# Products of 64 rows in the chunked linear attention of a four-stage kernel

## What is computed

```python
def step(S, inp):
    rt, dt, kt, vt, at, bt = inp
    sa = jnp.einsum('bhij,bhj->bhi', S, at)
    S = S * dt[:, :, None, :] + sa[..., None] * bt[:, :, None, :] + vt[..., None] * kt[:, :, None, :]
    y = jnp.einsum('bhij,bhj->bhi', S, rt)
    return (S, y)
```

## Time and profile before

| | |
|---|---|
| median of 3 runs | 3612.98 us (3612.59 to 3615.72) |
| the profiled execution's own time | 3623.5 us |
| its span, first to last instruction | 3621.8 us |
| mean granted clock of TensorE | 0.912 |
| TensorE busy | 3013.2 us (83%), 51,890 matmul records |
| VectorE busy | 2536.8 us (70%) |
| ScalarE busy | 1820.5 us (50%) |
| GpSimd busy | 1047.3 us (29%) |

### The profile page before, as it was taken

The page is one execution under the profiler, slowest core; times in us unless marked ns, Lnnn a source line. Parts: engine busy times, 40 slices in busy tenths (PEclk is TensorE's granted clock), DMA queues, the critical chain, the costliest instruction groups (busy, mean ns, idle before and its releaser), DMA issues.

```text
span 3621.8 us, 117698 instructions
## 1 busy us (share of the span) xinstructions
PE 3013.2 (83%) x51890; PEld 1965.8 (54%) x51890; DVE 2536.8 (70%) x5294; ACT 1820.5 (50%) x3063; POOL 1047.3 (29%) x1164
## 2 busy tenths in 40 slices
PE   6889999998648898988578888888888887779995
PEld 4555555555325555554245555555555555458774
DVE  3666666665549888888467777787777776457774
ACT  3334444444438878887244444454454552246661
POOL 0332122122531111222232332233333332045552
PEclk8899899899769999999789998899999997789997
DMA  2227999200043444330200000000000000056666
GB/s 75 79 97 304 395 394 319 30 1 1 33 138 128 137 143 140 129 126 21 70 3 4 12 11 9 10 10 13 10 10 10 10 12 14 9 190 228 224 214 180
DMA packets 161678, 356.92 MB, mean 99 GB/s; under 512 B 13821, under 2 KB 98559, under 8 KB 154896
## 3 DMA queue, kind: packets, MB, share of 16 engines
q1 hardware_dynamic: 147088, 323.95, 26.3%
q0 software_dynamic: 14080, 25.45, 2.1%
HBM read 136.33 MB, written 216.67 MB: 97 GB/s over the span
## 4 chain that ended last, share of the span: by engine, by line
PE 54%; DVE 21%; ACT 12%; issue 9%; DMA 2%; SPq 1%; another core or an unknown queue 1%; POOL 1%; DVEq 0%; POOLq 0%; ACTq 0%
PE ps L1551 7%; PE ps L135 4%; PE ps L137 4%; PE ps L136 4%; DVE t L485 3%; PE ps L1616 3%; PE ps L342 2%; PE ps L896 2%; ACT t L1035 2%; ACT t L1033 2%; PE ps L346 2%; PE ps L903 2%; PE ps L298 1%; PE ps L304 1%; DVE t L522 1%
## 5 line engine op out<-in xcount | busy, mean ns | idle before, releaser
L1551 PE MATMUL ps<-t 128*128 128x512 f32 x608 | 345.5, 682 | 49.7 <-DVE t L2056 13.0
L241 POOL TENSOR_SCALAR_AFFINE_SELECT t<-t 128x512 f32<-128x512 f32 x256 | 168.6, 659 | 663.4 <-ACT t L425 663.4
L485 DVE TENSOR_REDUCE t<-ps 128x2 f32<-128x512 f32 (+1 forms) x512 | 260.7, 551 | 116.5 <-PE ps L304 116.3
L135 PE MATMUL ps<-t 128*128 128x512 f32 (+1 forms) x660 | 280.6, 425 | 60.1 <-DVE t L511 34.9
L425 ACT ACTIVATE t<-ps 128x768 f32<-128x768 f32 x256 | 206.8, 808 | 213.1 <-PE ps L330 213.1
L137 PE MATMUL ps<-t 128*128 128x512 f32 (+1 forms) x660 | 258.5, 392 | 0.0
L136 PE MATMUL ps<-t 128*128 128x512 f32 (+1 forms) x660 | 258.2, 391 | 0.0
L1361 POOL DMA_INDIRECT deltas<-t x92 | 94.4, 1026 | 507.1 <-DVE t L1307 484.9
L2794 POOL DMA_INDIRECT answers<-t x156 | 153.9, 987 | 160.3 <-DVE t L2765 122.4
L1551 PEld LDWEIGHTS ps<-t 128*128 128x128 f32 x608 | 111.5, 207 | 142.9 <-issue 75.5
L135 PEld LDWEIGHTS ps<-t 128*128 128x128 f32 x660 | 128.4, 194 | 110.5 <-DVE t L511 42.9
(11 more groups left out here) (443 smaller groups left out, 8359.8 us busy)
## 6 DMA issues: line engine op xcount, KB each, us to landing
paired<-t SPq DMA_DIRECT2D x14, 8384.0 KB, 59.9
t<-experts SPq DMA_DIRECT2D x39, 1536.0 KB
sorted<-t SPq DMA_DIRECT2D x22, 1950.0 KB, 8.8
t<-in_wP SPq DMA_DIRECT2D x92, 320.5 KB, 3.5
experts<-t SPq DMA_DIRECT2D x8, 1536.0 KB, 6.0
t<-sorted SPq DMA_DIRECT2D x39, 260.0 KB
t<-answers SPq DMA_DIRECT2D x16, 512.0 KB, 6.7
t<-in_wE SPq DMA_DIRECT2D x8, 768.0 KB, 7.6
```

The lines of the kernel that those rows point to most:

```text
L135: pe.e.matmul(out, a[0], b[0], start=start, stop=False, skip_group_check=True)
L241: pool.e.affine_select(own, own, [[0, 2], [0, 2], [1, 128]], ALU.is_ge, 0.0, base=0, channel_multiplier=-1).then_inc(*kept(b, j))
L485: m = dve.e.tensor_reduce(nmf[:, z, blk * 16 + 4 * g + i0:blk * 16 + 4 * g + i0 + 2], ps[:, k:k + 2, a0:a1], AX.X, ALU.max, negate=True)
L1551: pe.e.matmul(ps[out, k, :], lhs, rhs, start=True, stop=True).then_inc(*e_pe(u, name))
```

## The change

The operands for b and k of a chunk now lie side by side (LB, BK, av, bk, each with an index of 2 before the 32 columns), so that one level product has 64 weight columns. Its result has b's rows in one quadrant of 32 partitions and k's in the next. The four chunks of a tile are numbered by bp and par: par picks the half of the partitions, bp a block of columns. What was in MT, TM, R and AV goes into one array T2, with a left and a right side of four blocks of 160 columns; the first 32 columns of the right side are the identity, written once at the start. The first square takes in the identity and has a third group of products, in place of VectorE's sum at L2196. AV and AP read and write quadrants 0 and 2 only. AP has one product of 128 columns where it had two of 64. TT takes two banks. The last step has three groups: one with 32 rows and 96 streamed columns, two with 64 rows, which sum over b and k in the array. ScalarE copies AP in three pieces and TT in two. GpSimd makes three more copies per half. AT, UNIT and HOLD stay as they are. The diff, cut to its core, with 8 columns of indentation less:

```diff
 Sx = sb([128, 3, 2, 64])
-LB = sb([128, 4, 2, 512])
+LB, BK = sb([128, 4, 16, 2, 32]), sb([128, 16, 2, 32])
 AR = sb([128, 5, 4, 2, 64])
 aR, rT = sb([128, 512]), sb([128, 2, 512])
-aT, bH, kH = (sb([128, 512]) for _ in range(3))
-MT = sb([128, 2, 2, 4, 32])
-TM = sb([128, 2, 4, 128])
-R = sb([128, 2, 2, 128])
-X1, AV, TT = sb([128, 2, 2, 32]), sb([128, 2, 2, 64]), sb([128, 2, 2, 32])
+av, bk = sb([128, 16, 2, 32]), sb([128, 16, 2, 32])
+T2 = sb([128, 2, 2, 4, 160])
+X1, TT = sb([128, 2, 4, 32]), sb([128, 2, 2, 2, 32])
 Z = sb([128, 2, 2, 2, 3, 32])
 hb = sb([128, 3])
...
     u, tile, y = k // 4, k % 4, k % 2
-    z, cols = u % 3, slice(k % 4 * 128, k % 4 * 128 + 128)
-    mtv, quads = MT[:, y, :, :, :], [slice(32 * i, 32 * i + 32) for i in range(4)]
-    own = [(h, q) for h in range(2) for q in quads]
+    z = u % 3
+    cells = [(h, bp, par) for h in range(2) for bp in range(2) for par in range(2)]
+    first = [slice(64 * par, 64 * par + 32) for par in range(2)]
+    second = [slice(64 * par + 32, 64 * par + 64) for par in range(2)]
+    both = [slice(64 * par, 64 * par + 64) for par in range(2)]
+    left, right = T2[:, y, 0, :, :], T2[:, y, 1, :, :]
+
+    def own(bp, par):
+        return second[par] if bp else first[par]
 
     def turn(n):
...
         for li in range(3 * s, 3 * s + 3):
-            for j in range(2):
-                at = j * 256 + li * 32
-                for i, q in enumerate(quads):
-                    ts = slice(tile * 128 + 32 * i, tile * 128 + 32 * i + 32)
-                    for h, hr in enumerate(heads):
-                        lhs = LB[hr, li, j, ts] if li < 4 else (bR2[hr, u % 2, ts] if j == 0 else kB[hr, z, ts])
-                        if li < 5:
-                            m = pe.e.matmul(by(ps[q, b + h, at:at + 32], 16), lhs,
-                                            AR[hr, li, tile, :, 16 * i:16 * i + 16], start=(li % 3 == 0 and j == 0),
-                                            stop=True, skip_group_check=True)
-                        else:
-                            m = pe.e.matmul(ps[q, b + h, at:at + 32], lhs, rB[hr, z, ts], start=False, stop=True,
-                                            skip_group_check=True)
+            for i in range(4):
+                bp, par, blk = i // 2, i % 2, 4 * tile + i
+                at = bp * 256 + li * 32
+                for h, hr in enumerate(heads):
+                    lhs = (LB[hr, li, blk, :, :] if li < 4 else BK[hr, blk, :, :]).rearrange("p j n -> p (j n)")
+                    if li < 5:
+                        m = pe.e.matmul(by(ps[both[par], b + h, at:at + 32], 16), lhs,
+                                        AR[hr, li, tile, :, 16 * i:16 * i + 16], start=(li % 3 == 0 and bp == 0),
+                                        stop=True, skip_group_check=True)
+                    else:
+                        m = pe.e.matmul(ps[both[par], b + h, at:at + 32], lhs,
+                                        rB[hr, z, blk * 32:blk * 32 + 32], start=False, stop=True,
+                                        skip_group_check=True)
         m.then_inc(*i_pe(k, "lev", s))
     elif s == 2:
         b = misc.take("tp", k)
         pe.wait_ge(*misc.free("tp", k))
         hold(b, HOLD["tp"][tile])
-        for n, src in enumerate((aT[:, cols], vB[:, z, cols], bH[:, cols], kH[:, cols])):
-            m = pe.e.transpose(ps[:, b, n * 128:n * 128 + 128], src, w["ident"])
+        for n, src in enumerate((av, bk)):
+            for bp in range(2):
+                to = ps[:, b, n * 256:n * 256 + 256].rearrange("p (h a n) -> p h a n", h=2, a=2)[:, :, bp, :]
+                m = pe.e.transpose(to, src[:, 4 * tile + 2 * bp:4 * tile + 2 * bp + 2, :, :]
+                                   .rearrange("p c j n -> p (c j n)"), w["ident"])
         m.then_inc(*i_pe(k, "tp"))
...
         pe.wait_ge(i_dve, k, "x0")
-        for h, q in own:
-            pe.e.matmul(ps[q, b, h * 64:h * 64 + 32], X1[q, y, h, :], mtv[q, h, 0, :], start=(h == 0), stop=True,
-                        skip_group_check=True)
-        for h, q in own:
-            m = pe.e.matmul(ps[q, b, h * 64 + 32:h * 64 + 64], mtv[q, h, 0, :], X1[q, y, h, :], start=False,
-                            stop=True, skip_group_check=True)
+        new = ps[:, b, 0:192].rearrange("p (h a n) -> p h (a n)", h=2, a=3)
+        for h, bp, par in cells:
+            pe.e.matmul(new[own(bp, par), h, 0:64], X1[first[par], y, 2 * h + bp, :],
+                        right[first[par], 2 * h + bp, 0:64], start=(h == 0), stop=False, skip_group_check=True)
+        for h, bp, par in cells:
+            pe.e.matmul(new[own(bp, par), h, 64:96], right[first[par], 2 * h + bp, 32:64],
+                        X1[first[par], y, 2 * h + bp, :], start=False, stop=True, skip_group_check=True)
+        for h, bp, par in cells:
+            m = pe.e.matmul(new[own(bp, par), h, 0:32], w["imask"][first[par], :], w["imask"][first[par], :],
+                            start=False, stop=True, skip_group_check=True)
         m.then_inc(*i_pe(k, "z", 1))
         b = misc.take("av", k)
         pe.wait_ge(i_act, k, "tm")
         pe.wait_ge(*misc.free("av", k))
-        for h, q in own:
-            m = pe.e.matmul(ps[q, b, h * 64:h * 64 + 64], mtv[q, h, 2, :], TM[q, y, 1, h * 64:h * 64 + 64],
-                            start=(h == 0), stop=True, skip_group_check=True)
+        for h, bp, par in cells:
+            n = 2 * h + bp
+            m = pe.e.matmul(ps[first[par], b, n * 64:n * 64 + 64], right[second[par], n, 32:64],
+                            left[second[par], n, 96:160], start=(h == 0 and bp == 0), stop=True,
+                            skip_group_check=True)
         m.then_inc(*i_pe(k, "av"))
...
     elif s == 7:
-        b, old = misc.take("tt", k), turn(4)
-        pe.wait_ge(*misc.free("tt", k))
+        old, b = turn(4), []
+        for bp in range(2):
+            b.append(misc.take("tt", k, bp))
+            pe.wait_ge(*misc.free("tt", k, bp))
         pe.wait_ge(i_act, k, "z", 4)
-        for h, q in own:
-            pe.e.matmul(ps[q, b, h * 32:h * 32 + 32], old[q, h, 2, :], old[q, h, 1, :], start=(h == 0), stop=False,
-                        skip_group_check=True)
-        for h, q in own:
-            m = pe.e.matmul(ps[q, b, h * 32:h * 32 + 32], w["imask"][q, :], old[q, h, 1, :], start=False,
-                            stop=True, skip_group_check=True)
+        for h, bp, par in cells:
+            q = own(bp, par)
+            pe.e.matmul(ps[first[par], b[bp], h * 32:h * 32 + 32], old[q, h, 2, :], old[q, h, 0, :],
+                        start=(h == 0), stop=False, skip_group_check=True)
+        for h, bp, par in cells:
+            q = own(bp, par)
+            m = pe.e.matmul(ps[first[par], b[bp], h * 32:h * 32 + 32], w["imask"][q, :], old[q, h, 0, :],
+                            start=False, stop=True, skip_group_check=True)
         m.then_inc(*i_pe(k, "tt"))
     elif s == 8:
         b = misc.take("ap", k)
         pe.wait_ge(*misc.free("ap", k))
-        pe.wait_ge(i_act, k, "tt")
+        pe.wait_ge(i_act, k, "tt", 1)
         pe.wait_ge(i_act, k, "av")
-        for h, q in own:
-            pe.e.matmul(ps[q, b, h * 128:h * 128 + 64], TT[q, y, h, :], TM[q, y, 0, h * 64:h * 64 + 64],
-                        start=(h == 0), stop=True, skip_group_check=True)
-        for h, q in own:
-            m = pe.e.matmul(ps[q, b, h * 128 + 64:h * 128 + 128], TT[q, y, h, :], AV[q, y, h, :], start=False,
-                            stop=True, skip_group_check=True)
+        for h, bp, par in cells:
+            n = 2 * h + bp
+            m = pe.e.matmul(ps[first[par], b, n * 128:n * 128 + 128], TT[first[par], y, bp, h, :],
+                            left[first[par], n, 32:160], start=(h == 0 and bp == 0), stop=True,
+                            skip_group_check=True)
         m.then_inc(*i_pe(k, "ap"))
...
         pe.wait_ge(i_dve, k, "lev", 5)
-        block = [(ch, h, quads[ch]) for ch in range(4) for h in range(2)]
-        for ch, h, tr in block:
-            pe.e.matmul(ps[heads[h], ch, 0:64], R[tr, y, h, 0:64], TM[tr, y, 2, heads[h]], start=True,
-                        stop=True, skip_group_check=True)
-        for ch, h, tr in block:
-            pe.e.matmul(ps[heads[h], ch, 128:160], R[tr, y, h, 0:64], mtv[tr, h, 1, :], start=False, stop=True,
-                        skip_group_check=True)
-        for ch, h, tr in block:
-            pe.e.matmul(ps[heads[h], ch, 64:128], TM[tr, y, 2, heads[h]], R[tr, y, h, 64:128],
-                        start=False, stop=False, skip_group_check=True)
-        for ch, h, tr in block:
-            pe.e.matmul(ps[heads[h], ch, 64:128], TM[tr, y, 3, heads[h]], TM[tr, y, 1, heads[h]],
+        block = [(ch, h, 2 * h + ch // 2, ch % 2) for ch in range(4) for h in range(2)]
+        for ch, h, n, par in block:
+            pe.e.matmul(ps[heads[h], ch, 64:160], left[first[par], n, 32:96], right[first[par], n, 64:160],
```

(50 more changed lines are left out.)

74 lines of the change are left out of this document (38 added, 36 removed).

## The result

The changed kernel takes 3532.13 us (3525.49 to 3539.58, four runs), the kernel before takes 3614.35 beside it: ratio 0.977, 95% interval 0.9747 to 0.9793, 82 us less. The direction that the prediction gave holds and 3532 lies in its range of 3525 to 3628, but the gain is twice the 40 us forecast. The profiled execution took 3525.49 us, with a span of 3523.7, so it is at the low end of its runs; 3623.5 before was 10.5 above the median, and the two profiles differ by 98 us.

What follows compares the result with a forecast made beforehand. TensorE was taken to bound the linear attention, its idle time mostly waits for instructions. Work +32, supply -80, new waits +5 and +3 sum to -40 us: from a median of 3612.98 to 3573, range 3525 to 3628.

Steps and rivals of the forecast that it cites:

- The bound: Linear attention stretch of 1302 us: TensorE, busy 1093 us, is the bound; most of its idle time awaits no data.
- Issue is the instruction supply: TensorE's issue waits, 134 us in the linear attention, mean that it has run ahead of its instruction fetches.
- Work, +32 us: TensorE's own time at full clock: levels -19, last step -8, AP +28, AV +15, first square +16 us.
- Supply, -80 us: TensorE's issue waits in the linear attention: 80 of 134 us go, with 24% fewer instructions.
- the two level lines: Issue waits at level products L1616 and L1620, 67.6 us: nearly all expected to go.
- a fifth of the other 66: Issue waits outside the level products, 66 us: only a fifth expected to go.
- The clock, 0 in the sum: TensorE work was priced at the full clock; the forecast sum has no term for clock changes.
- rival C: Nearly all issue waits go, 125 us, plus 10 us from fewer clock falls: -95, 3518 us; chance 0.08.
- New waits, +5 and +3: TensorE waiting behind ScalarE's extra copies, 5 us, and for TT's earlier reuse of ring banks, 3 us.
- A: Issue waits mostly stay, only the proportional 32 us go: +8, 3621 us; chance 0.16.
- B: Weight loads 64 wide run serially within a row group: level step 1.16 us, 3622 us in all; chance 0.07.
- D: Freed time is taken by waits for VectorE and ScalarE: 3605 to 3613 us, no change; chance 0.08.

Runs made afterwards that it cites:

- before_merged: Kernel before with the identity products of both heads merged in the turns and TT, 4,096 instructions less: 3532.48 us, ratio 0.985 on chip B.
- narrow_levels: Changed kernel with each level product split into b's and k's again, 12,288 instructions more: 3577.04 us, ratio 0.998 to the kernel before, chip B.
- narrow_again: Changed kernel with each level product split into b and k halves, 12,288 instructions more: 3641.83 us, ratio 1.0076 to the kernel before, chip E.
- merged_nohold: Changed kernel with merged identity products and without hold's unused products: 3537.16 us, ratio 0.9799 to the kernel before, chip C.
- after_merged: Changed kernel with both heads' identity products merged in first square, turns and TT, 5,120 instructions less: 3474.95 us, ratio 0.9681 to the kernel before, chip B.

## Why the prediction had the mechanism right, and where its size failed

**The bound.** Right. TensorE bounds the stretch and its issue waits were time on the path: they fell by 100 us and the stretch by 89.

**Issue is the instruction supply.** Right. The prediction rested it on one stall; 77 of the 80 longer issue waits end at the same distance behind a fetch. 226 fetches came as forecast, which only counts the instructions. `before_merged` has 5% fewer instructions and at most some 8 us less work, and gained 1.5% on two chips. `narrow_levels` and `narrow_again` bring the waits back with the instructions.

**Work, +32 us.** Right in its size. After the change the steps take 0.84, 0.97, about 0.5, about 0.5 and 1.09 us, against 0.84, 0.91, 0.46, 0.52 and 1.04. Medians over all steps without a wait inside, at the full clock, put single terms right: levels 0.95 to 0.83 us, -16 and not -19, since the 0.99 of the earlier trace rows was a long one; the last step 1.16 to 1.09, -5 and not -8; AP 0.47 to 0.97, +32 and not +28; first square and AV together 0.65 to 1.06, +27 and not +31. That is +38. The earlier trace rows answers with only +5. The difference is mostly the clock, below.

**Supply, -80 us.** The mechanism was right and the size too small: -100. The prediction gave the two level lines "nearly whole" and that held (67.6 to 3.2). It gave "a fifth of the other 66", 13 us, and more than half went: 30 are left. Of the waits that follow a fetch nearly all went, 116 to 5 us; what is left at the other lines is nearly all of the second kind, which rose from 19 to 28. `before_merged` shows why a fifth was too little: an edit of the turns relieves the level lines, so the waits are one account, and the prediction treated the lines one by one.

**The clock, 0 in the sum.** This is the step that failed most, a term that was put at nothing. The work was priced "at the full clock", and a gain of clock stood only in rival C, at 10 us, on the condition that nearly all issue waits go. Measured, 208 us at the half clock became 158, and 50 us less of it give back up to 25 us of busy time. This is an estimate from the price of about one half read above. With work of +38 it leaves +13 where +5 was measured, so some 8 us of busy time are not accounted for. On chip D, with both kernels on the same chip, the clock gives back some 54 us, more than the whole forecast gain. The time at the half clock follows the issue waits where both kernels or both forms ran (189 to 80 us on D, 300 to 171 on E), but it is not fixed by them, as `merged_nohold` shows.

**New waits, +5 and +3.** About right on chip A: the rest of the idle time went from 75 to 81. On chip D it went from 67 to 100, four times the term.

The sum, for the stretch: busy time +5 (work +30 to +38, the clock about -25 and the remainder), supply -100, waits +6: -89. The prediction had -40. The profiles differ by 98 us over the whole kernel, and by the medians it is 82. The 9 us outside the stretch are in code that the change hardly touches; over all the profiles here this part takes between 2300 and 2329 us, so they are no part of the gain that can be told from the spread.

**The rivals.** A, that only the proportional 32 us go, is refuted: 100 went. B, that weight loads of 64 columns run one by one within a row group at 48 ns, is refuted: the level step has 24 records per row group in 0.84 us, 35 ns each. The prediction found 57 ns for one such record on a tile; 24 of them one after the other would be 1.37 us, so the two tiles of one row group, which differ in their columns only, work beside one another for 64-wide weights too. The Trainium skill, page "TensorE: Matmul & The Clock Gate", section "Part 3: Packing small matmuls", lists the overlap of a weight load with running matmuls only for a different row group. For these tiles the trace disagrees. C was the nearest in mechanism: 100 of its 125 us went, nearly all of the waits that follow a fetch, and with them more clock than its 10; its 3518 was 14 us from the result, the forecast's 3573 41 us. It had been given 0.08. D, waits for other engines above 100 us, did not come on chip A (81), and came to its bound on chip D (100) without undoing the gain.

## What to carry to other kernels

Where TensorE runs many small products, count its instructions against the fetches of the queue "instruction". Idle time marked "issue" is supply where it ends at a fixed distance behind the end of a fetch, here 1.4 us. A wider or merged product relieves the lines around it too, so price the whole of such waits nearby and not the edited line alone. Then add the clock: shorter stalls also meant less time at 1.2 GHz, worth some 25 us beside 100 on chip A and 54 beside 108 on chip D. Merging products that share their weights was a 1.5% gain by itself, without any change of data layout.

## What the runs showed that was not expected

- The same two kernels gained 1.9, 2.2, 2.3 and 3.0% on four chips. The ratios 0.9809 and 0.9701 have intervals that do not meet, so a gain of this kind depends on the chip: by the profiles, in the issue waits left (35 and 6 us) and the time at the half clock (174 and 80). The issue waits that follow no fetch stand in every profile of chips A, C and E (14 to 29 us), where the kernel before takes 3614 us, and in none of chips B and D, where it takes 3583 and 3572. Why the chips differ so is open.
- The products without use paid for their time: without them the half clock went from 167 to 264 us, and the kernel was no faster with 19 us less of busy TensorE time.
- The narrow form was level with before on chip B (0.998) and slower on E (1.0076), with 180 and 300 us at the half clock.
- On chips A, C and E the remaining issue waits come in a regular form, one of 0.46 us after every four or five records of a group. The timeline of the changed kernel:

```profile
2002.34 0.26 PE L1650 MATMUL ps<-t 32*32 32x32 f32 x5 [0.46 <-issue]
2003.07 0.26 PE L1650 MATMUL ps<-t 32*32 32x32 f32 x4 [0.47 <-issue]
2003.79 0.18 PE L1650 MATMUL ps<-t 32*32 32x32 f32 x1 [0.46 <-issue]
```

With merged products they stand before L1660 instead on chips C and E (15 and 16 us), and on chip B `after_merged` has 1.8 us of issue in all. They come 0.73 us apart, while one fetch comes in 3.5 us, and 58 of the 70 issue waits left on chip A do not end behind a fetch as the others do. So they are not late fetches; what they are was not found.
